# Second attention with its rotated projections, row transposes and key spread in another order, and unused expert slots that read different rows

## The reference

```python
x = x + _L0_xattn_ref(_layernorm(x), ctx_1024, ctx_1024, mask_BxS2_bf0, ...)   # 16 heads of 8
x = x + _L0_ffn_ref(_layernorm(x), ...)     # 32 experts, top 4, swiglu, hidden 128
x = x + _L1_xattn_ref(_layernorm(x), ctx_1024, ctx_1024, ...)
x = x + _L1_ffn_ref(_layernorm(x), ...)     # 8 experts, top 2, silu, hidden 352
```

```python
Q = Q * cos + _rotate_half(Q) * sin
K = K * cos + _rotate_half(K) * sin
scores = jnp.einsum('bhtd,bhsd->bhts', Q, K) / jnp.sqrt(hd)
context = jnp.einsum('bhts,bhsd->bhtd', softmax(scores), V)      # then @ Wo + bo
...
y = jnp.sum(y.reshape(T, K, -1) * expert_weights[..., None], axis=1)
```

## Time and profile before

| | us |
|---|---|
| median of 3 runs (lowest, highest) | 1754.67 (1753.66, 1758.85) |
| the profiled execution: its time, its span | 1755.46, 1753.6 |
| first attention with its slots and inversion | 0 to 457 |
| first experts | 457 to 848 |
| second attention | 848 to 1297 |
| second slots and inversion | 1297 to 1363 |
| second experts | 1363 to 1753.6 |

### The profile page before, as it was taken

How to read it: one execution, slowest core, us unless ns; L and a number is a source line. 1 busy time by engine, 2 the same in 40 slices (tenths; PEclk the granted TensorE clock), 3 DMA queues, 4 the chain that set the end, 5 groups by cost and what they waited for, 6 DMA issues and landing times. The chain is left out here.

```text
span 1753.6 us, 56922 instructions
## 1 busy us (share of the span) xinstructions
PE 1360.9 (78%) x20300; PEld 1058.5 (60%) x20303; DVE 1170.2 (67%) x3429; ACT 956.9 (55%) x2354; POOL 1117.1 (64%) x1400
## 2 busy tenths in 40 slices
PE   5999999739677777776368788887854799999784
PEld 3677777514477667676246666665632588777663
DVE  5788888689577777776358888888869222322265
ACT  2677777627445555454156777776735344444332
POOL 3777777500477777775477778887410677777773
PEclk8999999969899999998669999999985899999988
DMA  4211111000144444447233222222100112112284
GB/s 164 85 45 36 45 36 46 21 7 1 33 107 108 103 108 106 105 109 83 69 92 125 64 62 63 63 63 60 36 17 1 49 54 55 54 53 54 55 216 150
DMA packets 136994, 122.85 MB, mean 70 GB/s; under 512 B 27675, under 2 KB 121915, under 8 KB 136123
## 3 DMA queue, kind: packets, MB, share of 16 engines
q0 software_dynamic: 26624, 56.35, 14.1%
q1 hardware_dynamic: 110078, 64.47, 12.1%
q10 hardware_dynamic: 192, 0.67, 0.1%
HBM read 80.24 MB, written 41.18 MB: 69 GB/s over the span
## 5 line engine op out<-in xcount | busy, mean ns | idle before, releaser
L1501 POOL DMA_INDIRECT arena<-expert_rows,token_of_slot x432 | 416.8, 965 | 281.7 <-issue 220.2
L419 POOL DMA_INDIRECT arena<-slot_results,slot x256 | 250.3, 978 | 104.5 <-issue 69.1
L1892 DVE TENSOR_TENSOR arena<-bank,arena 128x352 f32<-128x352 f32 x144 | 75.5, 524 | 223.1 <-ACT arena L1871 220.8
L1825 PE MATMUL bank<-W,arena 128*128 x576 | 196.8, 465 | 0.9 <-ACT arena L1883 0.9
L1736 POOL DMA_INDIRECT token_results<-arena,slot x144 | 141.1, 980 | 53.3 <-issue 41.4
L728 ACT ACTIVATE arena<-bank 128x512 f32<-128x512 f32 x256 | 132.1, 603 | 71.9 <-PE bank L910 59.2
L596 DVE TENSOR_REDUCE mx<-bank 128x8 f32<-128x512 f32 x256 | 158.4, 681 | 15.5 <-PE bank L873 12.6
L445 POOL TENSOR_TENSOR arena<-arena,fixed 128x1024 f32<-128x1024 f32 x64 | 121.3, 1916 | 46.0 <-ACT arena L746 46.0
L1599 PE MATMUL bank<-arena 128*128 128x128 f32 x1152 | 148.4, 285 | 0.0
L1599 PEld LDWEIGHTS bank<-arena 128*128 128x128 f32 x1152 | 141.5, 200 | 0.2
L1839 PEld LDWEIGHTS bank<-W,arena 128*128 128x128 f32 (+1 forms) x864 | 115.1, 192 | 37.9 <-issue 30.5
(11 more groups left out here) (215 smaller groups left out, 3349.8 us busy)
## 6 DMA issues: line engine op xcount, KB each, us to landing
slot_results<-arena SPq DMA_DIRECT2D x72, 256.0 KB, 2.5
arena<-in_ctx SPq DMA_DIRECT2D x64, 128.0 KB
expert_rows<-arena SPq DMA_DIRECT2D x64, 128.0 KB, 1.9
arena<-token_results SPq DMA_DIRECT2D x32, 256.0 KB, 4.1
arena<-expert_rows,token_of_slot POOLq DMA_INDIRECT x432, 2.6
W<-in_w SPq DMA_DIRECT2D x4, 1032.0 KB
X<-in_x SPq DMA_DIRECT2D x32, 128.0 KB, 2.2
arena<-slot_results,slot POOLq DMA_INDIRECT x256
```

Of the source, the lines that this page charges most:

```text
L419: nc.gpsimd.indirect_dma_start(out=gb[i.par][:, to:to + D], out_offset=None, in_=ys, in_offset=bass.IndirectOffsetOnAxis(ap=slot[:, at, k: ...
L1501: nc.gpsimd.indirect_dma_start(out=XE[n % R][:, c * ROW:(c + 1) * ROW], out_offset=None, in_=ts, in_offset=bass.IndirectOffsetOnAxis(ap=to ...
L1825: last = nc.tensor.matmul(H_[2 * r + u][:, 0:F1], XT[i.par][:, c * P:(c + 1) * P], W1a[:, bass.ds(x_e, 1), u * F1:(u + 1) * F1], start=Tru ...
```

## The change

In the second attention (L numbers of the kernel before):

- PE does the rotated projections right behind the plain ones, ahead of `maxima`; `rows_turned` moves from ahead of the maxima to behind `turned`, and waits until DVE has read the rotated projections out of the shared bank (`rot`); `next_values` goes ahead of `gate`.
- ACT has a body of its own, `body_with_spreads`: `normalise` goes ahead of the copies of maxima and of turned rows, the copy of turned rows goes behind that of the maxima, the spread of the keys ahead of the exponentials, that of the queries stays behind them.
- `keep_top` moves from POOL to ACT.
- DVE does `combine` and the statistics of its result ahead of `read_logits` and `add_output`.

In both inversions, a slot that no token has gets a row by its place (tile modulo 64, times 128, plus partition) instead of row 0. This adds an `iota` on POOL and two dependent operations on DVE in the first layer, one net in the second.

The diff, cut to its core:

```diff
@@ POOL, second attention
-                        if on(-4):
-                            keep_top(i.at(-4))
...
@@ DVE, second attention
+                        if on(3):
+                            combine(i.at(3))
                         if on(-3):
                             read_logits(p3)
                         if on(3):
-                            combine(i.at(3))
+                            hold(dve, s["combined"], i.at(3).n + 1)
+                            tile_stats(i.at(3), small["st_a"], "stats_a")
                         if on(-1):
                             add_output(pv)
...
@@ ACT, second attention
+                    def spread(i, dst, src, done):
+                        act.wait_ge(s["rope"], i.n + 1)
+                        for j in range(4):
+                            last = nc.scalar.activation(
+                                dst[i.par].rearrange("p (b j k) -> p b j k", b=4, j=4)[:, :, j, :],
+                                src[i.par].rearrange("p (b k) -> p b k", b=4), ACT.Copy,
+                                scale=head_of[:, j:j + 1])
+                        last.then_inc(s[done], 1)
...
+                    def body_with_spreads(i, on):
+                        ex, nx, old = i.at(2), i.at(1), i.at(-3)
+                        if on(1):
+                            inputs_copied(nx)
+                        if on(0):
+                            place_values(i)
+                        if on(-3):
+                            expert_rows(old)
+                        if on(2):
+                            normalise(ex)
+                        if on(-4):
+                            keep_top(i.at(-4))
+                        if on(0):
+                            maxima_copied(i)
+                        if on(-3):
+                            rows_copied(old)
+                        if on(1):
+                            spread(nx, Kbd, Kt, "kbd")
+                        if on(0):
+                            for r in range(UNITS):
+                                exps(i, r)
+                        if on(1):
+                            spread(nx, Qbd, Qt, "qbd")
@@ PE, second attention
                             projections(nx, P_, wq, wk, s["qk_psum"])
-                        if on(-3):
-                            rows_turned(p3)
+                            projections(nx, M_, Wm[:, 8, :], Wm[:, 9, :], s["rot_psum"])
...
                         if on(0):
                             maxima(i)
                             turned(i)
+                        if on(-3):
+                            if on(1):
+                                pe.wait_ge(s["rot"], nx.n + 1)
+                            rows_turned(p3)
                         if on(1):
-                            if on(-3):
-                                pe.wait_ge(s["tt"], p3.g + 1)
-                            projections(nx, M_, Wm[:, 8, :], Wm[:, 9, :], s["rot_psum"])
+                            next_values(nx)
                         if on(-3):
                             gate(p3)
-                        if on(1):
-                            next_values(nx)
@@ slots, POOL
+                    nc.gpsimd.iota(spread, pattern=[[0, -(-NT // TILES)], [P, TILES]], base=1, channel_multiplier=1,
+                                   allow_small_or_imprecise_dtypes=True).then_inc(slot_iota, 1)
@@ invert, DVE, second layer
-                        nc.vector.tensor_scalar(token_of_slot[:, 0:NT], found, -1.0, 0.0, ALU.add, ALU.max)
+                        link(nc.vector.scalar_tensor_tensor(offset, found, 0.5, spread[:, 0:NT], ALU.is_lt, ALU.mult))
+                        link(nc.vector.scalar_tensor_tensor(token_of_slot[:, 0:NT], found, -1.0, offset, ALU.add, ALU.add))
@@ invert, DVE, first layer
-                    nc.vector.tensor_scalar(token_of_slot[:, 0:NT], found, 0.0, None, ALU.max)
+                    link(nc.vector.scalar_tensor_tensor(offset, found, -0.5, spread[:, 0:NT], ALU.is_lt, ALU.mult))
+                    nc.vector.tensor_tensor(token_of_slot[:, 0:NT], found, offset, ALU.add)
```

More of the change, by code:

```diff
@@ L730, in projections @@
                     def projections(i):
-                        if layer:
-                            act.wait_ge(s["rope"], i.n + 1)
-                            for dst, src, done in ((Kbd, Kt, "kbd"), (Qbd, Qt, "qbd")):
-                                for j in range(4):
-                                    last = nc.scalar.activation(
-                                        dst[i.par].rearrange("p (b j k) -> p b j k", b=4, j=4)[:, :, j, :],
-                                        src[i.par].rearrange("p (b k) -> p b k", b=4), ACT.Copy,
-                                        scale=head_of[:, j:j + 1])
-                                last.then_inc(s[done], 1)
-                        else:
-                            if isinstance(i.n, int) and i.n == 0:
-                                act.wait_ge(const_in, 32)
-                                act.wait_ge(setup_pool, 2)
-                            act.wait_ge(s["qk_psum"], i.n + 1)
-                            nc.scalar.activation(Kt[i.par], P_[:, 2 * D:4 * D], ACT.Identity, bias=bk
-                                                 ).then_inc(s["keys"], 1)
-                            nc.scalar.activation(Qt[i.par], P_[:, 0:2 * D], ACT.Identity, bias=bq
-                                                 ).then_inc(s["queries"], 1)
@@ new lines, in projections @@
+                        if isinstance(i.n, int) and i.n == 0:
+                            act.wait_ge(const_in, 32)
+                            act.wait_ge(setup_pool, 2)
+                        act.wait_ge(s["qk_psum"], i.n + 1)
+                        nc.scalar.activation(Kt[i.par], P_[:, 2 * D:4 * D], ACT.Identity, bias=bk
+                                             ).then_inc(s["keys"], 1)
+                        nc.scalar.activation(Qt[i.par], P_[:, 0:2 * D], ACT.Identity, bias=bq
+                                             ).then_inc(s["queries"], 1)
@@ new lines, in keep_top, with rows_copied @@
+                    def keep_top(i):
+                        act.wait_ge(s["chosen"], i.g + 1)
+                        act.nop(nofuse=True)
+                        nc.scalar.activation(tiles(top, i), tp[i.par].rearrange("p (i e) -> p i e", i=2), ACT.Copy)
+                        nc.scalar.activation(tiles(top_at, i), ta[i.par].rearrange("p (i e) -> p i e", i=2), ACT.Copy
+                                             ).then_inc(s["top_kept"], 1)
+                    def rows_copied(i):
+                        act.wait_ge(s["tt_psum"], i.g + 1)
+                        nc.scalar.activation(tT[i.par], M_[:, 0:2 * D], ACT.Copy).then_inc(s["tt"], 1)
@@ L833, in body @@
                                 exps(i, r)
-                        if on(1) and layer:
-                            projections(nx)
-                        if on(2) and not layer:
+                        if on(2):
                             normalise(ex)
+                    def body_with_spreads(i, on):
+                        ex, nx, old = i.at(2), i.at(1), i.at(-3)
+                        if on(1):
+                            inputs_copied(nx)
+                        if on(0):
+                            place_values(i)
+                        if on(-3):
+                            expert_rows(old)
+                        if on(2):
+                            normalise(ex)
[4 more added lines that the diff above has]
+                        if on(-3):
+                            rows_copied(old)
+                        if on(1):
[5 more added lines that the diff above has]
+                            spread(nx, Qbd, Qt, "qbd")
                     if not layer:
                         constants["load_weights"](act)
-                    bodies(act, body)
+                    bodies(act, body_with_spreads if layer else body)
                 @block.tensor
@@ L1092, in inverse_iotas @@
         def inverse_iotas(K, NT):
-            return carve(NT * K, F16), carve(TILES // 4), carve(NT) if K == K1 else None
+            spread = carve(-(-NT // TILES) * TILES)
+            return carve(NT * K, F16), carve(TILES // 4), spread, carve(NT) if K == K1 else None
         def slots(layer):
@@ L1102, in slots @@
             place[0] = 0
-            iota_s, ids, unused = inverse_iotas(K, NT)
+            iota_s, ids, spread, unused = inverse_iotas(K, NT)
             oh = carve(TE * K, BF16)
```

28 lines of the change are left out of this document (10 added, 18 removed).

## The result

| | us |
|---|---|
| before, median (lowest, highest) | 1756.92 (1753.66, 1758.85), 19 runs |
| changed kernel | 1753.18 (1748.53, 1758.34), 19 runs |
| ratio, 95% interval | 0.9979, 0.9971 to 0.9988 |
| its profiled execution, span | 1748.74, 1746.9 |

The medians differ by 4 us where 14 were forecast. That is outside the range, and though the interval of the ratio leaves out 1, it is less than the 0.3% that the prediction took for a difference. The kernel's own runs spread over 10 us, and they go with the clock: over the 19, time and mean granted clock (TensorE's, as a share of full speed; 0.910 to 0.921) have a correlation of -0.85. The profiled execution is one of the shortest (clock 0.920), so its 6.7 us off the span are more than the medians give.

What follows compares the result with a forecast made beforehand. First experts paced by POOL's gathers with a slow DMA tail; second attention a 12.54 us loop with DVE, POOL near the limit. -8.2 + 1.1 - 6.5 - 2.3 + 2.3 = -13.6 us gives 1741 us, range 1725 to 1751.

Steps and rivals of the forecast that it cites:

- Tail of the first experts: End of first expert stage: unused slots read 128 different rows, last group starts earlier, -8.2 us (bounds 0 to -10.7).
- The added operations: Both inversions: two more dependent VectorE operations over 288 columns and one net over 144, exposed, +1.1 us.
- Rival (d): Spreading unused slots gives nothing, slow tail is from stores or the padding's number: 1749 us, chance 0.07.
- First body: Second attention's first body: rotated keys ready early, next scores begin at 901.3 instead of 903.6, -2.3 us.
- Last two: Second attention's last two bodies, without gathers: two periods of 12.3 instead of 22.30 us together, +2.3 us.
- Loop: Second attention: period falls from 12.54 to 12.3 us over 27 periods, -6.5 us (bounds -25 to +16).
- rival (c): Second attention slower: ACT's part late, PE's gaps cost clock, each period 0.8 us above 12.3: 1764 us, chance 0.06.
- The ring: Second attention: PE and ACT steps from one body's scores to the next sum to 12.2 to 12.36 us, limiting the period.
- Rival (b): Second attention's loop gains nothing, period 12.5, ACT's placing of values just late for the projections: 1747 us, chance 0.18.
- Rival (a): Second attention: neither ring closes, DVE runs at 11.6 us a period, -25.4 instead of -6.5: 1720 us, chance 0.15.
- VectorE at 12.2: Second attention: DVE's own loop, 11.6 plus 0.6 us, 0.5 of it an exposed wait before the residual addition.
- Copies on ACT: Second attention: the two small copies moved from POOL take 0.4 us a pair, hidden where ACT waits for the maxima.

Runs made afterwards that it cites:

- fill_ahead: Changed kernel plus five unneeded bf16 matmuls of 256 columns per body of the second attention, ahead of the output projection: 0.9892 of before, 1739.28 us.
- ring_off: fill_ahead plus one unneeded ACT activation (0.41 us) behind the query spread, ahead of the inputs' copy and the values' placing: 0.9889 of before.

## Why the prediction was wrong, step by step

- **Tail of the first experts**, -8.2: right; the last group's lag fell by 8.18 us, and the slots alone gave 0.9949. The added operations took 0.64 + 0.54 = 1.2 (forecast +1.1). Rival (d), that spreading does nothing, is out. The Trainium skill's price by size (DMA: Bandwidth & Descriptors, "Why small descriptors are slow (HBM only)") can't tell these two tails apart, since they fetch rows of one size; the measured shares, 0.92 and 0.38, decide.
- **First body**, -2.3: from the first maxima to the second scores 15.06 us became 12.88, 2.2 less, as forecast; the period lost 0.9 more since these scores ran 1.12 us instead of 2.01. **Last two**, +2.3: +2.2. Right.
- **Loop**, 27 x (12.54 - 12.3) = -6.5: **this is the step that failed**; +2.6 over 28 periods. The sum took all its durations from bodies at clock 1.00, and the new order takes that clock away. I did price PE's longer gaps at the lower clock, but only in rival (c), and there as a consequence of a late ACT. No late ACT was needed: with the wait ahead of the maxima gone, all of PE's waits stand in one stretch. The missing term is 28 x (12.71 - 12.28) = 12 us; the medians of changed kernel and `fill_ahead` differ by 14. That fillers in this stretch bring back clock and time is shown. That the clock fell because the waits stand together is argued from the rows; no run has the new order with its waits apart.
- **The count and the base** of that term were off as well: the earlier trace rows and the second body span 28 periods, not 27, and their mean before was 12.61, not the 12.54 of twelve of them. With both put right the term would be 28 x (12.61 - 12.3) = -8.7, and the forecast would have missed by more.
- **The ring**, 12.2 to 12.36: it measured 11.93 at full clock. The part from scores to turned rows was 7.40 us for a summed 7.65, and that from there to the next scores 4.53 for 4.71 without overlaps. The loop's 12.28 at full clock, so near to the forecast 12.3, is partly luck: VectorE makes it, by its reading of the rotated projections, for which PE waits and which the ring left out, and by its 0.30 us in every second body.
- **Rival (b)**, loop gains nothing, was forecast at 1747 and is nearer to the measured time than the sum, but by the wrong cause: ACT's placing of the values isn't late, as `ring_off` shows. **Rival (a)**, a period of 11.6, didn't come even at full clock, and **rival (c)**, above 12.96, didn't either.
- **VectorE at 12.2**: 0.5 us ahead of the residual addition, as forecast (0.54); at full clock its bodies take 12.1, and 12.4 where the 0.30 ("issue") comes in.
- **Copies on ACT** 0.4 a pair, hidden: 0.20 each, hidden; but moving them off POOL was worth 0.4% on the old order (0.9949 to 0.9909), half of it at the end of the attention. The changed kernel has that end too (-3.0 in the table); the prediction had no term for it.
- What stays open: by what measure the clock falls; the runs show only at which orders it fell and with what work it came back. The new place of the rotated projections was tried with VectorE's old order only with fillers, not without them. The slots alone save 9 us and the order alone costs 2.4, but both together save 3.7 and not 6.6; 0.9949 x 1.0014 is 0.9963 where 0.9979 was measured, and by the three intervals that difference isn't clear of noise. What lengthened the stretch behind the last maxima by 1.6 us wasn't looked into.

The best versions beat both kernels: five short unneeded matmuls in each body bring the changed kernel to 1739.3 us, 1.1% below the one before, and without unneeded work the old order with spread slots and the copies on ACT stands at 1741.9.

## What to carry to other kernels

A sum over a ring holds only at the clock of its rows: when a change takes a wait of PE away, look where PE's remaining waits come to lie, and price PE's part of the ring at the lower level as a rival of its own. Follow every semaphore that a moved step waits for, and put it into the ring. Measure the parts of a change apart; here the 9 us of one part hid that the other lost some. Read a transfer's price from the share and rate of its stretch, not from its bytes, when many packets ask for one row.

## What the runs showed of the hardware

- In the tail of the first experts, where the unused slots all read one row: 73 GB/s at a DMA share of 0.92; with rows spread, 104 GB/s at 0.38.
- A tensor engine busy 0.82 of the loop (123.09 of 150.48 us) kept the clock at 1.00, and one busy 0.84 (128.06 of 153.27, part of it at the lower level) did not. What the rows show to differ is where its waits lay, not that they were longer in all.
- At the lower level the scores' 32 matmuls took 1.95 us instead of 1.12, and a body at clock 0.87 took 0.5 us more than one at 1.00.
- Sixty more bf16 matmuls of 256 columns in twelve bodies made the loop 6.1 us shorter.
- From VectorE's last choice of experts to the next block's first operation it took 3.60 to 3.90 us with the last small copies on GpSimd and 0.88 with them on ScalarE.
